# Gathered embedding rows of all four batch tiles in SBUF at once, with weight rings of four pieces

## What is computed

```python
sparse_embed = emb_tables[field_idx[None, :], x_sparse]      # 512 x 26 x 64
z = sparse_embed.reshape(B, N_FIELDS * K)
gram = jnp.einsum('bik,bjk->bij', sparse_embed, sparse_embed)
iu, ju = jnp.triu_indices(N_FIELDS, k=1)
inner = gram[:, iu, ju]
dnn_in = jnp.concatenate([x_dense, z, inner], axis=-1)
h = jax.nn.relu(dnn_in @ w1 + b1)                            # w1 is 2002 x 2002
out = jax.nn.sigmoid(h @ w2 + b2)
```

## Time and profile before

| what | value |
|---|---|
| time, median of 3 runs | 332.91 us (328.24, 332.91, 335.99) |
| span of the profiled execution | 328.7 us |
| PE busy | 245.6 us, 75% |
| DVE busy | 143.8 us, 44% |
| ACT busy | 138.9 us, 42% |
| POOL busy | 108.1 us, 33% |
| moved by DMA | 36.16 MB, mean 110 GB/s |
| mean granted TensorE clock | 0.834 of full speed |

### The profile page before, as it was taken

One profiled execution on the slowest core, in us unless ns is written; L12 is line 12 of the kernel. 1 busy time (PEld: TensorE's weight loads), 2 busy tenths in 40 slices (PEclk: granted clock), 3 DMA queues, 4 the chain that ended last, 5 costly groups with the idle time before them and its releaser, 6 DMA issues.

```text
span 328.7 us, 3445 instructions
## 1 busy us (share of the span) xinstructions
PE 245.6 (75%) x1110; PEld 198.8 (60%) x1110; DVE 143.8 (44%) x315; ACT 138.9 (42%) x334; POOL 108.1 (33%) x115
## 2 busy tenths in 40 slices
PE   6673041000345969597999999999999999999995
PEld 5452030000234857475798888888887887888884
DVE  4420040000044756584655986444456564744413
ACT  4411020001025645463455798767755561544420
POOL 6777777777346667675200000000000000000000
PEclk9785557555556998989667899999999999999999
DMA  6773335368215778667023245333310214560000
GB/s 206 210 224 80 27 28 151 26 152 214 22 33 138 202 197 212 205 154 209 10 49 138 62 129 185 124 103 116 108 53 1 64 43 146 156 221 0 2 0 0
DMA packets 13719, 36.16 MB, mean 110 GB/s; under 512 B 3511, under 2 KB 4811, under 8 KB 13598
## 3 DMA queue, kind: packets, MB, share of 16 engines
q1 hardware_dynamic: 9622, 29.79, 28.0%
q0 software_dynamic: 3792, 6.12, 12.9%
q10 hardware_dynamic: 288, 0.03, 0.1%
HBM read 34.55 MB, written 1.39 MB: 109 GB/s over the span
## 4 chain that ended last, share of the span: by engine, by line
PE 61%; another core or an unknown queue 24%; ACT 5%; DMA 4%; issue 3%; DVE 2%; POOL 1%; SPq 0%; ACTq 0%; DVEq 0%
PE bank L620 46%; PE bank L602 11%; ACT w_hi L451 3%; PE bank L588 3%; DMA E<-emb,row_idx 2%; DMA gram_dram<-G 1%; POOL E L415 1%; ACT ET L461 1%; DMA x_in<-gram_dram 1%; ACT x_hi L456 1%; DMA x_idx<-x_sparse 1%; DVE G L529 0%; SPq L390 0%; DVE bank L550 0%
## 5 line engine op out<-in xcount | busy, mean ns | idle before, releaser
L620 PE MATMUL bank<-w_hi,x_hi 128*128 128x500 f32 (+4 forms) x256 | 113.4, 443 | 72.4 <-issue 57.4
L415 POOL DMA_INDIRECT E<-emb,row_idx x104 | 103.6, 997 | 51.7 <-issue 28.9
L620 PEld LDWEIGHTS bank<-w_hi,x_hi 128*128 128x128 f32 (+2 forms) x256 | 52.5, 205 | 90.1 <-issue 78.1
L620 PE MATMUL bank<-w_lo,x_hi 128*128 128x500 f32 (+4 forms) x256 | 106.1, 415 | 0.0
L620 PE MATMUL bank<-w_hi,x_lo 128*128 128x500 f32 (+4 forms) x256 | 106.0, 414 | 0.0
L507 DVE TENSOR_TENSOR w_lo<-w_raw,w_hi 128x502 fp32r<-128x502 f32 (+1 forms) x104 | 65.3, 679 | 16.8 <-ACT w_hi L451 16.3
L516 DVE TENSOR_TENSOR x_lo<-bank,x_hi 128x128 fp32r<-128x128 f32 x52 | 14.9, 291 | 116.5 <-issue 66.1
L451 ACT CAST w_hi<-w_raw 128x502 fp32r<-128x502 f32 (+1 forms) x104 | 57.3, 611 | 17.0 <-PE bank L620 15.8
L456 ACT CAST x_hi<-bank 128x128 fp32r<-128x128 f32 x52 | 13.8, 266 | 113.7 <-remote 84.0
L620 PEld LDWEIGHTS bank<-w_hi,x_lo 128*128 128x128 f32 (+2 forms) x256 | 52.2, 204 | 11.2
L620 PEld LDWEIGHTS bank<-w_lo,x_hi 128*128 128x128 f32 (+2 forms) x256 | 52.7, 206 | 8.0
(11 more groups left out here) (25 smaller groups left out, 27.1 us busy)
## 6 DMA issues: line engine op xcount, KB each, us to landing
w_raw<-w SPq DMA_DIRECT2D x26, 501.0 KB
w_raw<-w SPq DMA_DIRECT2D x26, 500.0 KB
E<-emb,row_idx POOLq DMA_INDIRECT x104
gram_dram<-G SPq DMA_DIRECT2D x4, 338.0 KB
w_all<-w SPq DMA_DIRECT2D x1, 1001.0 KB, 4.5
x_in<-gram_dram SPq DMA_DIRECT2D x8, 58.5 KB
x_in<-gram_dram SPq DMA_DIRECT2D x4, 45.5 KB
x_idx<-x_sparse SPq DMA_DIRECT2D x1, 52.0 KB, 1.8
```

What stands on the lines that cost most here:

```text
L415: nc.gpsimd.indirect_dma_start(out=E[:, t, bt % 2, f, :], out_offset=None, in_=emb_rows, in_offset=bass.IndirectOffsetOnAxis(ap=at, axis=0 ...
L620: last = nc.tensor.matmul(bank[b0 + q][:, 0:CHUNKS[h][q][1]], x, w[:, cols], start=(t == 0 and m == 0), stop=(t == NT - 1 and m == 2))
```

## The change

`E` gets four places instead of two, one for each batch tile, so that a gather overwrites nothing. The wait of POOL on `e_transposed` goes, and each place of `E` has a counter of its own for landing. To make room, the rings of weights have four places instead of five: RAW and HL are 4. `make_steps` computes its list from both, so the places of splits and loads in STEPS move as well. No other instruction is added or removed.

```diff
-RAW = 5
-HL = 5
+RAW = 4
+HL = 4
...
-        E = sb("E", [P, ZT, 2, 2, K], F32)
+        E = sb("E", [P, ZT, BT, 2, K], F32)
...
-        e_landed = [[sem(f"e_landed{t}_{r}") for r in range(2)] for t in range(ZT)]
+        e_landed = [[sem(f"e_landed{t}_{r}") for r in range(BT)] for t in range(ZT)]
...
             for k, (bt, t) in enumerate(GATHERS):
-                if bt >= 2:
-
-                    pool.wait_ge(e_transposed, transposed_count(bt - 2, t))
                 for f in range(2):
                     at = row_idx[:, bt, 2 * t + f:2 * t + f + 1]
                     nc.gpsimd.indirect_dma_start(
-                        out=E[:, t, bt % 2, f, :], out_offset=None, in_=emb_rows,
-                        in_offset=bass.IndirectOffsetOnAxis(ap=at, axis=0)).then_inc(e_landed[t][bt % 2], 16)
+                        out=E[:, t, bt, f, :], out_offset=None, in_=emb_rows,
+                        in_offset=bass.IndirectOffsetOnAxis(ap=at, axis=0)).then_inc(e_landed[t][bt], 16)
...
                     bt, t = step[1:]
-                    pe.wait_ge(e_landed[t][bt % 2], 32 * (bt // 2 + 1))
+                    pe.wait_ge(e_landed[t][bt], 32)
                     wait_aux(step)
-                    nc.tensor.transpose(bank[aux(step)][:, 0:P], E[:, t, bt % 2, :, :].rearrange("p f k -> p (f k)"),
+                    nc.tensor.transpose(bank[aux(step)][:, 0:P], E[:, t, bt, :, :].rearrange("p f k -> p (f k)"),
                                         ident[:]).then_inc(e_transposed, 1)
```

## The result

The changed kernel takes 386.48 us, median of 4 runs (383.31 to 388.9), the kernel before 333.71 us (328.24 to 335.99, 4 runs). The ratio is 1.169, with a 95% interval from 1.153 to 1.185. The profiled execution of the changed kernel took 384.78 us with a span of 383.0 us, 54.3 us longer than the span of before.

A forecast was written before the change was run, and what follows sets the result against it. PE bounds the kernel, its updates held back while POOL gathers without pause. 328.7 + 38.4 (longer hold-up) - 10.0 (idle given back) + 8 (rings) = 365, plus half of a 4.2 us difference to the median: 367 us, range 332 to 386.

The forecast's parts named there:

- the upper sum of the prediction: Whole kernel: 386 us, with release 7.9 for 1.2, +6 for a round, rings +12 for +8, the 4.2 whole.
- a round lost by PE: Held stretch: if the pace of updates doesn't stay, PE is one round less far when POOL ends, +6 us.
- the hold-up ends by itself: Rival: PE leaves the hold-up near 94 us as now, whatever POOL's pauses; 331 us, chance 0.15.
- Faster: Rival, 86 to 161 us: the two-way tie of POOL and PE holds PE, not gathers; 314 us, chance 0.11.
- milder: Rival: after the large w1 gathers near 66 us updates pass every 2 us; 344 us, chance 0.12.
- the 40 us more: Casts of x_hi, up to 138 us: they wait 40 us more in all for "remote".
- The pace of the held updates: While POOL gathers without pause: PE's updates come out in PE's order, 9.0 us each.
- The release after POOL's last instruction: After POOL's end at 138.5 us: the waiting cast follows 1.2 us later, at most 7.9 us.
- the shift up to the 12th transpose: Held stretch: 138.5 + 1.2 - 101.3 = +38.4 us, PE at 138.5 standing where it stood at 101.3.
- The 10 us given back: Between 101.3 and 161.5 us: with POOL silent, PE's 10.0 us of idle time can go, -10.0.
- Rings of four, +8: Eight rounds before the gram matrices: the smaller ring leaves PE 1.5 us short per round; +8, bounds 0 and 12.
- the two terms: The -10.0 us of PE idle time given back and the +8 us for rings of four.

The follow-up runs named there:

- places4_wait: Changed kernel with POOL's wait on the transposes put back: 335.85 us, ratio 1.021 to the kernel before (334.18 us).
- unread_gathers: Changed kernel with all transposes reading one constant block, gathers issued but unread, SP's waits for landed gathers out: 382.23 us, ratio 1.160 to the kernel before.
- no_gathers: unread_gathers without the 104 gathers, the three of w1 rows kept: 266.09 us, ratio 0.808 to the kernel before.
- pool_memsets: unread_gathers with each gather replaced by a POOL memset of 1300 columns of E: 269.83 us, ratio 0.819 to the kernel before.
- plain_pool_dmas: unread_gathers with each gather replaced by a plain POOL DMA of the same size: 266.22 us, ratio 0.808 to the kernel before.
- rings4: Kernel before with rings of four instead of five, POOL's wait and two places of E kept: 335.44 us, ratio 1.017.
- half_gathers: unread_gathers with only the gathers of batch tiles 0 and 1: 260.87 us, ratio 1.022 to the kernel before (256.63 us).
- fifth set: Changed kernel run again on another chip: 265.33 us against 257.39 us for the kernel before, ratio 1.035; half_gathers repeated there: 262.26 us.
- before_fill128: Kernel before with a POOL memset of 128 floats behind each gather: 262.33 us, ratio 1.019 to the kernel before (256.63 us).
- after_fill128: Changed kernel with a POOL memset of 128 floats behind each gather: 266.89 us, ratio 1.044 to the kernel before (256.63 us).
- after_fill1: Changed kernel with a POOL memset of 256 floats behind each gather: 267.41 us, ratio 0.813 to the kernel before (328.69 us).
- before_fill1: Kernel before with one POOL memset of 256 floats behind each gather: 269.88 us against 328.69 us for the kernel before.

## Why the prediction was right in kind and short by 19 us

The measured 386.48 us lies just above the range, whose end is 386. That the upper sum of the prediction, also 386, comes so close is luck: it has a round lost by PE, which didn't come, 7.9 us for the release and 12 for the rings, and leaves out POOL's later end and the longer gram stretch.

**Direction and mechanism: shown where updates are held.** Gathers without pause hold PE's updates back, and the change removes the pause. places4_wait gives the time back by that wait alone, unread_gathers and no_gathers show that it is the gathers and not the rows, pool_memsets and plain_pool_dmas that it is neither a busy POOL nor its DMAs as such. The rival "the hold-up ends by itself" (331 us) falls where updates are held: there updates come late to the last gather and beyond. The sentence cited with it, the Trainium skill's "PE and ACT never wait on anyone" (SBUF - State Buffer, section Who interferes with whom), stands in a section on the engines' ports to SBUF. The prediction stretched it to the time at which PE's results are seen, and so stretched it doesn't agree with the 382 against 266 us of unread_gathers and no_gathers; of the ports these runs say nothing. "Faster" and "milder" fall as well: with POOL's wait gone, the late casts wait for 125.0 us in place of 84.0, the 40 us more that the prediction named.

**The pace of the held updates: forecast a little too slow.** The forecast had 8 casts done and the 9th transpose waiting when POOL ends; in the trace 9 are cast and 11 have run. POOL ended at 141.1 instead of 138.5, as some gathers took longer than 0.94 us (mean 0.980).

**The release after POOL's last instruction: the step that failed.** I took 1.2 us, at most 7.9. The 10th cast came 8.5 us after POOL's end (149.61 - 141.06), the 11th 13.5. In sum, the shift up to the 12th transpose is 49.2 us where the prediction has 38.4, 10.8 short. POOL's later end is 2.6 of it (141.06 - 138.5). The other 8.2 lie between that end and the 12th transpose: 18.95 us (160.01 - 141.06), where the forecast has 10.7 (1.2, and 9.5 from 101.3 to 110.82), although PE had come further. I had the larger value in hand, 86.00 to 93.90, and chose the smaller since it stood at the end of the hold-up. The long pauses of places4_wait and rings4 agree with the larger: from the end of the last gather to the cast it is 8.3 us (100.30 - 92.05) and 6.8 (98.80 - 91.99), and at the end of unread_gathers even 13.4 (154.15 - 140.79). What sets this length isn't settled; half_gathers was for that and fell on a chip where nothing is held.

**The 10 us given back: 6.0 of them came back.** I took PE's idle time between 101 and 161 us for small hold-ups that go with POOL. Between the 12th and the 24th transpose of the kernel before this is right: PE idles twice, 6.0 of 35.52 us in all, each time behind a cast that waited for "remote".

```profile
119.33 0.27 ACT L456 CAST x_hi<-bank 128x128 fp32r<-128x128 f32 x1 [4.42 <-remote]
...
120.77 0.47 PE L620 MATMUL bank<-w_hi,x_hi 128*128 128x502 f32 x1 [2.53 <-DVE x_lo L516]
```

The other is 3.4 us ahead of the product at 139.24, behind the cast at 137.79. With POOL silent both are gone. Of the other 4.0 us, 1.3 are the end of the idle time up to 102.59, ahead of this stretch, and 2.7 fall at the start of the gram matrices, where no cast of `x_hi` is waited for. What PE idles in the changed kernel instead, 8.6 of 37.24 us, is the ring alone, once in each of the six rounds:

```profile
165.68 0.50 PE L617 MATMUL bank<-w_hi,x_hi 128*128 128x502 f32 x1 [1.43 <-DVE w_lo L504]
```

**Rings of four, +8: right in size.** In the result each of the seven rounds behind the hold-up waits 1.43 us for `w_lo`, 10.0 us in all, where I had worked out 1.5 for each of eight. Where nothing is held, the changed kernel's whole loss is 7.9 us (265.33 - 257.39), but that this is the 8 of the sum is chance: there 11 rounds wait 1.45 us each (15.9 / 11), and not all of the 15.9 us is loss, since a PE that waits for the ring waits less for rows. Two kernels with the same memset behind each gather show it. PE waits 14.3 us for rows with rings of five (before_fill128); with rings of four (after_fill128) it waits 15.7 us for `w_lo` and 3.1 for rows. 15.7 + 3.1 - 14.3 = 4.5 us, and the medians lie 4.6 apart (266.89 - 262.33). In the result, between the 12th and the 24th transpose, the ring's 8.6 us, the 6.0 given back and 0.8 less of busy time make the 1.7 us above. The sum has -2 for the two terms, so this is 3.7 us of the miss, most of it the 4.0 us that were no such hold-up or lay ahead.

**The gram stretch** isn't in the prediction: 4.0 us longer at a granted clock of 0.62 against 0.71, for the same 141 matmuls. I didn't find out why the clock is lower there. The remaining parts are -0.6 elsewhere and 1.4 from the span to the median (386.5 - 383.0 = 3.5 where the forecast has 2.1). The sum is 10.8 + 3.7 + 4.0 - 0.6 + 1.4 = 19.3 of the 19.5 us (386.5 - 367).

**What the prediction couldn't know** is that the mechanism isn't always present. In the fifth set the same change is +3.5%, not +16.9%. The sign is the same in both comparisons of the two kernels.

**The best version.** Where updates are held, after_fill1 and before_fill1 beat both kernels, 267.41 and 269.88 us against 328.69; where they aren't, the kernel before is best (257), and the closest fill that was run there costs it 1.9% (before_fill128, with gathers 1.33 us apart at the closest, less than the 1.45 shown to free the updates). Between 262 and 270 us on either sort of chip, a kernel with a fill is the safer one. before_fill1 itself wasn't run where nothing is held.

## What to carry to other kernels

When a matmul's consumer starts late and nothing shown ended its wait, compare its start with the matmul's own end before you look for a slow engine, and look at which queue works without a pause meanwhile. A wait on an engine off the critical path can be worth time to the others by the pause that it makes, so before removing one, ask what runs back to back without it. A result from one chip is one sample: a kernel whose time hangs on such an effect should be timed on several, and the cheap spacing (0.33 us on POOL per gather, here 104 gathers) weighed against the 1.9% that it cost the kernel before where it wasn't needed.

## What the runs showed of the hardware

- Indirect DMAs that POOL issued 1.25 us apart held the updates of PE's matmuls back, by up to 47 us from a transpose's end to its cast, in three sets and in the first comparison, and not at all in two other sets. At 1.45 us apart, with a memset of 0.33 us between, nothing was held (265.6 us span against 370.4 on the same chip). Anything between is open.
- The hold-up can repeat exactly: one distance from cast to cast was 36.40 us in four traces. Where POOL paused, the next one was 12.60 or 10.50 us in place of 19.60.
- After the last gather the held updates took 8.5 and 13.5 us more, with POOL silent and DVE and ACT nearly idle; after the first long pause of POOL it took 6.8 to 8.3 us in three traces.
- 104 plain DMAs from POOL, 0.65 us each, and memsets of 1.2 us end to end did nothing of the kind.
- The kernel before took 257 us in two sets, each on its own chip, and 329 to 334 in the other comparisons, with a spread of 3 to 4% in each set: 70 us and more, where the change costs 53 us in the one sort and 8 us in the other.
